# The token-major copy of x in a fused Mamba and ternary-FFN kernel: block transposes on VectorE and a way through DRAM in place of transposes on TensorE

## What is computed

```python
zxbcdt = einsum('bld,ed->ble', u, W_in)          # z | x, B, C | dt
dt  = softplus(zxbcdt[..., -8:] + dt_bias)
xBC = silu(causal_conv4(zxbcdt[..., 1024:2176]) + conv_b)
y   = ssd(x, dt, -exp(A_log), B, C) + x * D      # state-space scan, 8 heads of 128
yg  = y * silu(z)
x1  = layernorm(u + (yg * rsqrt(mean(yg**2) + eps) * norm_w) @ W_out.T)
wu, wg, wd = ternary(W_up), ternary(W_gate), ternary(W_down)
out = layernorm(x1 + (silu(x1 @ wu.T) * (x1 @ wg.T)) @ wd.T)
```

## Time and profile before

| | us |
|---|---|
| median of the three runs shown | 1471.48 |
| their lowest and highest | 1470.85, 1477.58 |
| the profiled execution's own time | 1473.74 |
| its span in the trace | 1471.7 |
| TensorE matmuls busy | 1447.2 |
| TensorE weight loads busy (beside the matmuls) | 1303.3 |
| VectorE / ScalarE / GpSimd busy | 1016.4 / 861.0 / 432.1 |

### The profile page before, as it was taken

The page is one execution under the profiler, slowest core; times in us unless marked ns, Lnnn a source line. Parts: engine busy times, 40 slices in busy tenths (PEclk is TensorE's granted clock), DMA queues, the critical chain, the costliest instruction groups (busy, mean ns, idle before and its releaser), DMA issues.

```text
span 1471.7 us, 26863 instructions
## 1 busy us (share of the span) xinstructions
PE 1447.2 (98%) x10132; PEld 1303.3 (89%) x10132; DVE 1016.4 (69%) x2219; ACT 861.0 (59%) x1655; POOL 432.1 (29%) x544
## 2 busy tenths in 40 slices
...
GB/s 272 65 48 97 101 52 80 87 101 84 65 98 87 80 86 55 99 100 59 87 132 255 108 115 123 166 136 167 112 179 101 158 122 165 130 126 169 100 136 66
DMA packets 141760, 168.05 MB, mean 114 GB/s; under 512 B 76480, under 2 KB 85184, under 8 KB 141632
## 3 DMA queue, kind: packets, MB, share of 16 engines
...
HBM read 132.62 MB, written 33.69 MB: 113 GB/s over the span
## 4 chain that ended last, share of the span: by engine, by line
PE 89%; DMA 4%; DVE 3%; ACT 2%; issue 1%; SPq 1%; POOL 0%; DVEq 0%; ACTq 0%
PE ps L403 25%; PE ps L265 23%; PE ps L473 16%; PE ps L359 11%; PE ps L313 3%; PE ps L393 3%; DMA x_scratch<-s_rr 2%; PE ps L321 2%; PE ps L330 2%; PE ps L300 1%; DVE s_xact L841 1%; SPq L1406 1%; PE ps L233 1%; PE ps L286 1%; DMA s_rr<-in_un 0%
## 5 line engine op out<-in xcount | busy, mean ns | idle before, releaser
L403 PE MATMUL ps<-s_xoh,s_S 128*128 128x256 f32 x896 | 220.3, 281 | 0.1
L403 PE MATMUL ps<-s_xol,s_S 128*128 128x256 f32 x896 | 220.3, 282 | 0.0
L473 PE MATMUL ps<-s_tern,s_hh 128*128 128x512 f32 x504 | 199.2, 395 | 0.0
L473 PE MATMUL ps<-s_tern,s_hl 128*128 128x512 f32 x504 | 199.2, 395 | 0.0
L265 PE MATMUL ps<-s_uhi,s_whi 128*128 128x256 f32 x1088 | 180.7, 288 | 2.7 <-ACT s_uhi L543 2.7
L403 PEld LDWEIGHTS ps<-s_xoh,s_S 128*128 128x128 f32 x896 | 169.5, 189 | 5.9 <-issue 0.9
L265 PE MATMUL ps<-s_uhi,s_wlo 128*128 128x256 f32 x1088 | 174.5, 283 | 0.0
L265 PE MATMUL ps<-s_ulo,s_whi 128*128 128x256 f32 x1088 | 174.1, 282 | 0.0
L403 PEld LDWEIGHTS ps<-s_xol,s_S 128*128 128x128 f32 x896 | 169.4, 189 | 4.8
L1284 POOL TENSOR_TENSOR s_lnb<-s_lnb,s_cst 128x1 f32<-128x1 f32 x32 | 18.2, 572 | 497.0 <-DVE s_lnb L1131 497.0
L403 PE MATMUL ps<-s_xol,s_tern 128*128 128x256 f32 x672 | 163.7, 281 | 0.0
...
## 6 DMA issues: line engine op xcount, KB each, us to landing
s_S<-wsum_scratch SPq DMA_DIRECT2D x48, 512.0 KB, 3.6
s_S<-wsum_scratch SPq DMA_DIRECT2D x96, 256.0 KB, 3.4
s_bcx<-ct_scratch SPq DMA_DIRECT2D x32, 512.0 KB, 3.8
s_wst<-in_wffn SPq DMA_DIRECT2D x48, 256.0 KB, 2.8
...
s_uraw<-in_uT SPq DMA_DIRECT2D x16, 512.0 KB, 6.4
s_rr<-in_un SPq DMA_DIRECT2D x32, 256.0 KB, 3.1
x_scratch<-s_rr SPq DMA_DIRECT2D x32, 256.0 KB, 2.2
```

The source lines that it names most:

```text
L403: o = e.matmul(bank[:, 256 * mi:256 * mi + 256], wt(mi, k), xo[g % 2][:, x, k, :], start=(first and mi == 0 and k == 0 and xo is xoh), sto ...
L473: o = e.matmul(DB[c][:], y[:, 128 * c:128 * c + 128], tern[:, j, 1024:1536], start=(j == 0 and lo == 0), stop=(j == 15 and lo == 1))
```

## The change

TensorE's transposes `TR` and ScalarE's copies `f_xTe` are removed. Instead VectorE turns the 32x32 blocks of `xact` into a new buffer `xs` (`f_xtr(c, a)`, two per chunk), SyncE stores `xs` to DRAM in four DMAs (`store_xb`) of 128-byte pieces so that the blocks come to their places, and loads the whole with one DMA of 512 KB into `xT` (`load_xT`), which has two buffers now. `f_xtr` of the next chunk waits until those four stores have landed; `load_xT` waits for them too, on SyncE's queue, and for the Y and xw that used the buffer.

The dt products go to B0[1], a bank of Y, instead of MISC: DT waits for the gate of the chunk before, CUM takes over the waits for MISC, and Y waits until `f_dtr` has read the bank. In the order `dtT(m)` stands directly behind `DT(m)`.

ScalarE normalises x1 (`f_x1`), as x·r + (-mean·r); GpSimd's `f_rs1` computes the second factor in a further step. For chunks 12 to 31 the turned x1 isn't made in the first stage: in the Strassen stage, `load_xr` reads the stored chunk back into `xtt`, `f_xt2` turns it, and `store_xt2` stores it, one chunk every two steps Q from Q = 0 to 40; `load_xt(g, i)` waits for these from g = 3 on.

All five orders are written anew, the start's too; the splits of the input weights are shared out differently (VectorE takes eight of 17 instead of two).

```diff
-    xT, o_xT = sb("xT", [128, 3, 8, 128])
+    xT, o_xT = sb("xT", [128, 2, 8, 128])
+    xs, _ = sb("xs", [128, 4, 8, 32])
...
+    xtt, _ = sb("xtt", [128, 512], F32, o_dts)
...
+    xbd = nc.dram_tensor("xb_scratch", [32, 32, 4, 8, 4, 32], F32, kind="Internal").ap()
...
-    DVE_LO = [8, 12]
+    DVE_LO = [16, 8, 11, 15, 13, 12, 7, 6]
...
+    def xT_landed(w, c):
+        w.wait_ge(d_xT[c % 2], 16 * (c // 2 + 1))
+    def x1_count(c):
+        return sum(80 if i < 12 else 16 for i in range(c % 3, c + 1, 3))
     def x1_stored(w, c):
-        w.wait_ge(d_x1[c % 3], 80 * (c // 3 + 1))
+        w.wait_ge(d_x1[c % 3], x1_count(c))
...
         def DT(m):
-                w.wait_ge(s_ms, 4 * m - 2)
-                w.wait_ge(s_GM, 2 * m)
+                w.wait_ge(s_gate[1], 4 * m - 2)
-                i = e.matmul(MISC[32 * k:32 * k + 32, :]...
+                i = e.matmul(B0[1][32 * k:32 * k + 32, :]...
...
         def Y(c):
             w.wait_ge(s_DI, c + 1)
-            later = c + 1 if c % 2 else c + 2
+            xT_landed(w, c)
             for half in range(2):
-                w.wait_ge(s_xTe[half], later)
-                if c % 2:
-                    w.wait_ge(s_gate[half], c)
+                w.wait_ge(s_gate[half], c)
+            if c == 0 or c % 4 == 2 and c < NCH - 2:
+                w.wait_ge(s_neg, (c + 2) // 4 + 1)
...
TensorE, the step of m:
-            DT(m); OP(c - 1); ip(n, 0); ip(n, 1); dtT(m); ip(n, 2); Y(c); CUM(m); ip(n, 3); ST(c); G(n); ip(n, 4)
-            ip(n, 5); OP(c); Y(c + 1); SQ(c); ip(n, 6); ip(n, 7); ip(n, 8); TR(c + 2, 1); TR(c + 2, 0); ST(c + 1)
-            TR(c + 3, 0); SQ(c + 1); TR(c + 3, 1); OP(c + 1); ip(n + 1, 0); ip(n + 1, 1); ip(n + 1, 2); Y(c + 2)
-            ip(n + 1, 3); ip(n + 1, 4); ST(c + 2); G(n + 1); ip(n + 1, 5); OP(c + 2); Y(c + 3); SQ(c + 2)
-            ip(n + 1, 6); ip(n + 1, 7); ST(c + 3); TR(c + 4, 1); TR(c + 4, 0); ip(n + 1, 8); TR(c + 5, 0); SQ(c + 3)
-            TR(c + 5, 1)
+            DT(m); dtT(m); ip(n, 0); ip(n, 1); OP(c - 1); ip(n, 2); Y(c); CUM(m); ip(n, 3); ST(c); G(n); ip(n, 4)
+            OP(c); Y(c + 1); SQ(c); ip(n, 5); ip(n, 6); ip(n, 7); ip(n, 8); ST(c + 1); SQ(c + 1); OP(c + 1)
+            ip(n + 1, 0); ip(n + 1, 1); ip(n + 1, 2); ip(n + 1, 3); Y(c + 2); ip(n + 1, 4); ip(n + 1, 5); G(n + 1)
+            ST(c + 2); OP(c + 2); Y(c + 3); SQ(c + 2); ST(c + 3); ip(n + 1, 6); ip(n + 1, 7); ip(n + 1, 8); SQ(c + 3)
...
ScalarE:
+        def f_x1(c):
+            v, r = lnb[:, c % 2, :], rr[:, c % 3, :]
+            w.wait_ge(s_rs1, 2 * c + 2)
+            e.activation(r, r, AF.Identity, scale=v[:, 11:12], bias=v[:, 12:13]).then_inc(s_x1, 1)
...
VectorE:
+        def f_xtr(c, a):
+            w.wait_ge(s_silc, 5 * (c // 2) + 2 * a + 3)
+            if c:
+                w.wait_ge(d_xb, 64 * c)
+            e.transpose(xs[:, :, 4 * a:4 * a + 4, :].rearrange("p i h b -> p h i b"),
+                        xact[:, 4 * a:4 * a + 4, 128 * (c % 2):128 * (c % 2) + 128].rearrange(
+                            "p h (i t) -> p h i t", i=4)).then_inc(s_xtr, 1)
...
+        def f_xt2(c):
+            w.wait_ge(d_xs, 80 * (c - 12) + 16)
+            e.transpose(xtt[:], xtt[:]).then_inc(s_xt, 1)
...
VectorE, the start and the step of m:
+        f_xtr(0, 0); split_in(7); split_in(6); f_xtr(0, 1); split_out(0); skip_diag(); split_out(1); f_xtr(1, 0)
+        f_xtr(1, 1); f_ulo(1); f_dd(0); f_GM(0); f_dd(1); split_out(2); f_M(0); ...
...
+            f_ms(c - 1); f_dte(m); f_ulo(n)
...
+            f_taps(n, 4); f_gate(c + 1, 0); f_xtr(c + 2, 0); f_xtr(c + 2, 1); f_dd(c + 2); f_gate(c + 1, 1)
+            f_xtr(c + 3, 0); f_ms(c); f_xtr(c + 3, 1); f_sqsum(c + 1); f_r1(c); f_ms(c + 1); f_dd(c + 3); f_ulo(n + 1)
...
+            f_xtr(c + 4, 0); f_ms(c + 2); f_gate(c + 3, 0); f_gate(c + 3, 1); f_r1(c + 2); f_xtr(c + 4, 1)
...
+            f_S(c + 3); f_xtr(c + 5, 0)
...
+            f_xtr(c + 5, 1)
...
GpSimd:
         def f_xw(c):
             w.wait_ge(s_wz, c + 1)
-            w.wait_ge(s_xTe[0], c + 1)
-            w.wait_ge(s_xTe[1], c + 1)
+            xT_landed(w, c)
...
+            e.tensor_scalar(v[:, 12:13], v[:, 8:9], v[:, 11:12], -1.0, mult, mult).then_inc(s_rs1, 1)
...
+            f_Cexp(c + 3); f_edge(n + 1, 1); f_Sd(c + 2); f_edge(n + 1, 2); f_xw(c + 3)
...
+            f_edge(n + 1, 3); f_ygl(c + 2); f_DI(c + 3); f_edge(n + 1, 4); f_rs(c + 2); f_rs1(c + 1); f_Sd(c + 3)
...
SyncE:
+        def load_xr(c):
+            x1_stored(w, c)
+            w.wait_ge(s_dtT, NG // 2)
+            w.wait_ge(d_ct, 16 * (NG // 2))
+            w.wait_ge(d_xs, 80 * (c - 12))
+            e.dma_start(xtt[:], x1d[128 * c:128 * c + 128, :]).then_inc(d_xs, 16)
+        def store_xt2(c):
+            w.wait_ge(s_xt, c + 1)
+            for i in range(4):
+                e.dma_start(xtd[c // 2, :, :, 4 * (c % 2) + i, :],
+                            xtt[32 * i:32 * i + 32, :].rearrange("a (f b) -> a f b", b=32)).then_inc(d_xs, 16)
...
+        def store_xb(c):
+            w.wait_ge(s_xtr, 2 * c + 2)
+            for j in range(4):
+                e.dma_start(xbd[c, :, :, :, j, :].rearrange("a i h b -> a (i h) b"),
+                            xs[32 * j:32 * j + 32].rearrange("p i h b -> p (i h) b")).then_inc(d_xb, 16)
+        def load_xT(c):
+            w.wait_ge(d_xb, 64 * c + 64)
+            if c >= 2:
+                w.wait_ge(s_Y, c - 1)
+                w.wait_ge(s_xw, c - 1)
+            e.dma_start(xT[:, c % 2].rearrange("p h s -> p (h s)"),
+                        xbd[c].rearrange("a i h j b -> i a (h j b)")).then_inc(d_xT[c % 2], 16)
...
SyncE, the step of m:
+            load_r0(c)
+            if m <= 3:
+                store_xt(c - 2)
+            load_wst(3 * n + 1); load_bc(c + 2); store_xb(c + 2); load_wst(3 * n + 2); load_xT(c + 2); load_bc(c + 3)
+            store_xb(c + 3); load_wst(3 * n + 3); store_x1(c - 1); load_r0(c + 1); load_bc(c + 4); load_wst(3 * n + 4)
+            load_bc(c + 5)
+            if m <= 3:
+                store_xt(c - 1)
+            load_xT(c + 3)
...
+            store_x1(c + 1); store_xb(c + 4); load_r0(c + 3); load_xT(c + 4); store_x1(c + 2); store_xb(c + 5)
...
+            load_wst(3 * n + 6); load_xT(c + 5)
...
```

More of the change, by code:

```diff
@@ L852, in f_dte @@
             w.wait_ge(s_negA, 1)
-            e.tensor_scalar(dts[:], MISC[:], dtb[:, 8:9], None, add).then_inc(s_dte, 1)
+            e.tensor_scalar(dts[:], B0[1][:], dtb[:, 8:9], None, add).then_inc(s_dte, 1)
         def f_dtr(m):
@@ L1141, in program_dve @@
-        f_sqsum(0); f_GM(1); f_taps(1, 3); f_taps(1, 4); f_gate(1, 0); f_gate(1, 1); f_ms(0); f_dd(2); f_wz(1)
-        f_sqsum(1); f_r1(0); f_dd(3); f_x1(0); f_S(1)
+        f_ulo(0); split_in(16); setup(); f_taps(0, 0); f_dte(0); split_in(8); split_in(11); f_dtr(0); split_in(15)
+        f_dA(0); split_in(13); split_in(12); f_cte(0); f_taps(0, 1); f_taps(0, 2); f_taps(0, 3); f_taps(0, 4)
+        f_xtr(0, 0); split_in(7); split_in(6); f_xtr(0, 1); split_out(0); skip_diag(); split_out(1); f_xtr(1, 0)
@@ L1144, in program_dve @@
+        f_xtr(1, 1); f_ulo(1); f_dd(0); f_GM(0); f_dd(1); split_out(2); f_M(0); split_out(4); f_taps(1, 0); f_M(1)
+        f_wz(0); f_taps(1, 1); f_taps(1, 2); f_GM(1); split_out(7); f_gate(0, 0); split_out(3); f_wz(1); f_gate(0, 1)
+        split_out(5); f_S(0); f_xtr(2, 0); f_dd(2); split_out(6); f_sqsum(0); f_taps(1, 3); f_taps(1, 4); f_ms(0)
+        f_gate(1, 0); f_gate(1, 1); f_xtr(2, 1); f_sqsum(1); f_r1(0); f_xtr(3, 0); f_dd(3); f_xtr(3, 1); f_S(1)
         for m in range(1, NG // 2):
@@ L1145, in program_dve @@
             n, c = 2 * m, 4 * m - 2
-            f_ms(c - 1); f_ulo(n); f_dte(m); f_M(c); f_taps(n, 0); f_dtr(m); f_wz(c); f_dA(m); f_taps(n, 1)
-            f_gate(c, 0); f_gate(c, 1); f_cte(m); f_wz(c + 1); f_taps(n, 2); f_M(c + 1); f_GM(n); f_r1(c - 1)
-            f_sqsum(c); f_S(c); f_xt(c - 2); f_taps(n, 3); f_taps(n, 4); f_gate(c + 1, 0); f_dd(c + 2)
-            f_gate(c + 1, 1); f_x1(c - 1); f_ms(c); f_sqsum(c + 1); f_dd(c + 3); f_xt(c - 1); f_r1(c); f_S(c + 1)
-            f_ulo(n + 1); f_ms(c + 1); f_M(c + 2); f_wz(c + 2); f_taps(n + 1, 0); f_taps(n + 1, 1); f_taps(n + 1, 2)
@@ L1182, in program_dve @@
                 f_h21(Q - 1); f_h12(Q - 1)
+            if Q % 2 == 1 and Q < 40:
+                f_xt2(12 + Q // 2)
             if p == 2:
@@ L1331, in program_pool @@
             e.memset(xact[:, 2 * k:2 * k + 2, 256:259], 0.0).then_inc(s_zero, 1)
-        split_in(16); f_Cexp(0); split_in(9); split_in(11); split_in(10); split_in(13); split_in(2); split_in(14)
-        split_in(15); split_in(0); split_in(1); split_in(3); f_edge(0, 0); split_in(6); f_edge(0, 1); split_in(5)
-        f_edge(0, 2); split_in(4); f_edge(0, 3); f_edge(0, 4); split_in(7); f_DI(0); f_xw(0); f_edge(1, 0); f_Cexp(1)
-        f_DI(1); f_edge(1, 1); f_edge(1, 2); f_ygl(0); f_edge(1, 3); f_edge(1, 4); f_xw(1); f_rs(0); f_rs1(0); f_Sd(1)
@@ L1423, in load_xt @@
             X, kh, h = XQ[i]
```

(7 more changed lines are left out.)

231 lines of the change are left out of this document (116 added, 115 removed).

## The result

The changed kernel takes 1539.13 us (median of four runs, 1536.32 to 1541.04) against 1472.99 for the kernel before: a ratio of 1.0443, 95% interval 1.041 to 1.0476. The forecast was 1450.5 and a range that ends at 1477; it is slower by 66 us, where a gain of 21 was forecast. The profiled execution took 1537.49 us, its span is 1535.6.

The account below looks back on a forecast made before the run. TensorE's nearly hole-free list of work was taken as the bound. Terms -30 - 5 + 6 + 2 + 3 + 3 = -21 us gave 1452.7 against the profiled 1473.7, hence 1450.5 us against the median; range 1437 to 1477, the forecast's own 1444 to 1464.

Parts of the forecast that it names:

- the load behind the round: First stage, 512 KB load of xT after the four stores: landing between 3.8 and 6.4 us, +3 us (0 to 10).
- SyncE's other waits have room: SyncE's DMA queue in the first stage: what it loads is used a half step on; no cost added.
- TR, -30: First stage, TensorE: the 256 removed transposes take 27.9 to 31.4 us off its list; -30 us taken.
- DT's old waits, -5: DT no longer waits for f_ms (3.1 us), and the slow output projection behind one wait recovers 1.7: -5 us for both.
- dtT behind DT, +6: Seven new places where TensorE idles 0.87 us while VectorE adds the bias between DT and dtT: +6 us, a floor.
- The round, +2: VectorE waits for a chunk's four stores to land before the next block transposes: 5.8 us each, costing +2 us overall.
- The start and the end of the stage: Start: f_ulo(1) queued behind chunk 0's stores, +3 us. First stage's end: Y(30), Y(31) wait for loads, 0 (-4 to +4).
- Strassen, 0 to 2: Strassen stage: 20 moved x1 transposes (14 us) and their 100 DMAs lie beside TensorE's list: 0, at most 2 us.
- rival 3: First stage: waiting for a chunk's stores takes its upper bound, 8.8 us, opening TensorE holes: 1496.5 us; chance 0.13.
- Rival 2: First stage: the stores take 6.5 to 7.5 us, as with doubled issue time: 1459 to 1473, taken as 1469; chance 0.15.
- Rival 4: DMA rings become the bound: a chunk's 4096 pieces take over 24.7 us; at 30 us the whole takes 1640; chance 0.02.
- the prediction's estimate of 62 us: Draining a chunk's stores, 3.3 us by the rows, would take 62 by the skill page's factor 19; whole some 2680 us.

## Why the prediction was wrong

**The step that failed** is the load behind the round: "The load behind it, 512 KB: between the 3.8 us of bcx and the 6.4 of uraw". Both prices are those of other DMAs of the same size; this one has the slowest dimension 4, and it took 8.6 to 14.6 us from its issue to the start of xw. In four parts with the slowest dimension 32 it took 4.3 to 7.8 at the same eight places. The prediction saw that "xw waits for it, and f_ygl and f_DI, which OP and Y wait for, are queued behind xw", but with the wrong duration it got +3, at most 10; xw made late by itself measured 49. "So the landing is covered" failed once, for Y at the end of the stage (6.9 us). The sentence "SyncE's other waits have room: what it loads is used a half step on" failed with it: the queue behind a slow copy measured 51 through bcx and f_zs. With the load in four, and nothing else changed, the kernel stands at 1455.2, inside the forecast's own range of 1444 to 1464. Those of its other terms that could be measured fit within 3 us each (below).

**How 84 us come together.** Over the span the changed kernel leaves TensorE idle for 88.2 us, the load in four for 34.4 (1452.3 - 1417.9): 54 more. The rest is the clock: the mean granted clock is 0.975 in the trace of the changed kernel and 0.995 with the load in four, 38 and 7 us short of full clock, an estimate from each span times what is missing. Here it falls behind idle times of TensorE, though not behind each (below): the stretch from 238 to 242 us, above, has 0.59, and four matmuls take 1.05 instead of 0.64 us in it, that is 1.2 instead of 2.4 GHz. The prediction priced holes by their length alone, although the kernel before has such a case in the earlier trace rows: the output projection that took 7.34 us instead of 5.60 stands behind an idle of 1.99, and the granted clock from 567 to 570 us is 0.50 of 2.4 GHz:

```profile
565.27 1.07 PE L233 MATMUL ps<-s_uraw,s_wdr 128*32 128x512 f32 x8 [1.99 <-DVE s_lnb L970]
566.27 3.40 PE L359 MATMUL ps<-s_wohi,s_ygh 128*128 128x512 f32 x8
...
571.65 2.02 PE L359 MATMUL ps<-s_wohi,s_ygl 128*128 128x512 f32 x8
```

The prediction put the 1.7 us "to the wait as well", as part of its -5, and gave no hole of its own such a second price.

**Term by term**, on the run with the load in four:
- TR, -30: 28.3 measured. DT's old waits, -5: none of the DTs in the steps waits; the one wait left, 2.7 us, is that of DT(0) in the start. The term was not tried by itself.
- dtT behind DT, +6: eight waits of 8.2 us in all, seven of them in the steps; the size was right, but the wait lay over another of nearly the same length, and undoing it gained nothing that can be seen.
- The round, +2: from the first issue (233.27) to the next block transpose (238.74) it took 5.5 us in the changed kernel, where 5.8 was taken; the other rounds that VectorE waited for took 5.5 to 7.0. With the load in four, OP waited for f_r1 2.8 us in all. Block transposes took 0.698 us, 0.707 were taken.
- xw behind the load in four, +3: it waits 4.5 us at most, and none of it reaches TensorE's waits; Y waits once for a load, 2.9 us, at the end of the stage.
- The start and the end of the stage: DT(1) starts at 83.22 us as before (83.24), so the start lost what the transposes of its four chunks had cost, 4 x 0.87 = 3.5 us by the prediction's price, where +3 was taken. The end of the stage, 0 with 4 on either side: 6.95 us idle in 686 to 790 against 5.65.
- Strassen, 0 to 2: 593.4 us against 592.6.

The rivals of the prediction: rival 3 came out on the right side for the wrong reason. No round that VectorE waited for took its 8.8 us, and its two places cost little. Rival 2's long issues were there (5.34 us), but the median issue is 0.67 us, and the longest come behind the load. Its times are 2 us too high: 7 to 21 us beside the +2 give 1457.5 to 1471.5. Rival 4's bound was not reached: with 128-byte pieces a store lands in 3.5 us, with 1 KB rows in 2.6, and the time is the same. The Trainium skill, page "VectorE: DVE Perf Modes", section "The three transpose paths", gives its factor of 19 for a large innermost stride at the destination, and against the crossbar's time. The pieces here are 128 bytes in a row, so the prediction's estimate of 62 us used the factor on a pattern for which the page doesn't give it; no run here tests the factor itself. What no rival had was a load that is slow by its own pattern, although its pattern stood in the diff.
